# Two gated linear attention layers: half-chunk decay sums taken as rows, and a new order of work on three engines

## The chip, the cores and the metric

One core of a Trainium2 chip runs the whole program in one launch. The metric is device time in microseconds of one execution. Before the change three runs took 3049.61, 3051.63 and 3058.26 us.

## The reference

The program computes eight residual blocks on x of 2048 tokens by 128 features: an attention, a gated linear attention with experts (`L0_ffn`), a second attention, `L0_ffn` again, a selective scan, a mixture of experts, a gated delta rule, and the mixture of experts again. The change is in `L0_ffn` alone, which occurs twice with the same weights. Cut to what matters:

```
q1, k1, v = x@Wq * s, x@Wk, x@Wv              # 8 heads of 64
q2 = x@Wqa@Wqb * s ;  k2 = softmax(x@Wka@Wkb)
gk1 = log_sigmoid(x@Wg1a@Wg1b + bg1) / 16     # log decays <= 0
gk2 = log_sigmoid(x@Wg2a@Wg2b + bg2) / 16
e = softmax(x@We) ; one of 4 experts per token: mask, weight
chunk_gla(q, k, v, gk):                       # chunks of 64 tokens
    g = cumsum(gk) in the chunk ; qg = q*exp(g) ; kg = k*exp(-g)
    o = tril(qg kg^T) v  +  qg S
    S = S * exp(g_last) + (k*exp(g_last-g))^T v
o = chunk_gla(q1,k1,v,gk1) + sum over experts of
    chunk_gla(q2*w_e, k2*w_e, v, gk2*mask_e)
o = o * rsqrt(mean(o*o) + eps) * norm_w * silu(x@Wga@Wgb)
x = x + o @ Wo
```

## The kernel before, in words

`gla_ffn` (from line 790) handles the 2048 tokens in 16 tiles of 128. Its state has five parts: one dense and one for each of four experts. The kernel centres the cumulated log decays on the middle of a tile: `cum` sums them from the middle row. What crosses from one tile to the next is then the state times the exponential of the second half sum of the last tile and the first half sum of this one. These two half sums, for 512 key columns and five states, are the subject of the change.

- `halves(t)` (line 998, TensorE): for each of four groups of 128 key columns the log decays `gk` are the stationary operand (128x128 float32), and two columns (dense) or eight columns (four experts, two halves) stream past. That is eight small matrix products a tile, each of two passes, and they put the key columns on partitions, where `state_decay` needs them. The first four lie between `intra` and the expert part of `inter`, the last four between that and `update`.
- `exp_half(t)` (line 1440, ScalarE) takes the exponential of 128x40 numbers; `state_decay(t)` (line 1287, VectorE) multiplies the second half of the last tile with the first half of this one; `decay_state(t)` (POOL) scales the state by it.

Every engine has its program order written out by hand in the loops over t at the ends of `on_pe`, `on_dve`, `on_act`; semaphores join them. While tile t is finished, the front of tile t+1 is made (values, keys, queries, their decays) and the gate logits of t+2. TensorE's loop, in the names that are used below: `scores(t,0)` (line 1040, dense), `cumulate(t+1)` (988), `scores(t,1)` (experts), `spread_experts(t)` (1057, the expert mask over all partitions), `values`, `low_keys`, `low_queries`, `inter(t,(0,))` (1066, the old state's part of the output), `gate_logit(t+2,0)` and `(t+2,1)` (975), `gate_project(t+1)` (965), `intra(t)` (1083), halves, `inter(t,1..4)`, halves, `update(t,0)`, `update(t,1)` (1093), `keys`, `queries`, `sum_squares` (1108), `turn_k0`, `turn_q0` (transposes, 1019), `update_dense` (1100), `turn_k1`, `turn_q1`, `project` (1113).

VectorE's loop: `state_decay`, `mask_scores(t,0)`, `mask_scores(t,1)` (1292), `mask_queries(t)` (1300, 2048 columns), `subtract_max`, `normalise_keys`, `expert_queries`, `finish_gates(t+2)` (1241), `weigh_gate(t+1)` (1236), `add_state` twice, `decay_keys`, `dense_queries`, `add_state_dense`, `normalise`, `add_x`.

PSUM: three banks serve as a ring, whose order of uses is the list `TILE_USES`; a use may start when the reader of the use three places ahead of it has finished. `Dbank`, an eighth bank, holds in turn the spread masks, the output gate's logits (read by `weigh_gate`), and the dense part of the state's update.

```
TILE_USES = "cum0 cum1 klow v q2 half g0 g1 k1 q1 rs tk0 tq0 tk1 tq1 out".split()
```

In tiles 2 to 4 masks of later tokens are turned and multiplied as well, at the end of tile 1 VectorE chooses the experts of the last 1536 tokens, and in tile 0 the norm of the last 1024 tokens is finished.

## Time and profile before

| | |
|---|---|
| median of three runs | 3051.63 us |
| the profiled execution's own time | 3046.48 us |
| its span, first to last instruction | 3045.0 us |
| TensorE busy | 2802.7 us (92%) |
| VectorE busy | 2489.2 us (82%) |
| ScalarE busy | 2064.8 us (68%) |
| POOL busy | 858.6 us (28%) |
| first linear attention, start of its norm to its last x | 656.2 to 1068.7 us |
| second one, its last x | 2133.3 us |
| ScalarE exp_halves, line 1443 | 32 of 185 ns |

In a row of the timeline the first number is the start in us, the second the busy time of the group, then engine (PE a matmul, PEld its weight load), line, operation, output <- inputs, shapes and count, and in brackets the idle time ahead of it with what ended it. A float32 product shows as two weight loads and two matmuls. PEld's starts are the surest clock of TensorE's order: the time from the first load of one step to the first load of the next is what the step takes.

### The profile page before, as it was taken

Reading aid. Unit: us, or ns where it says so; the run is one execution under the profiler, and the core shown is the slowest. Engines: PE = TensorE matmul, PEld = TensorE weight load, DVE = VectorE, ACT = ScalarE, POOL = GpSimd, SP = SyncE. Lnnn points to the kernel's source line nnn. Section 1 sums busy time; section 2 is a strip of 40 time slices with the busy share of each in tenths; the row PEclk is TensorE's granted clock in tenths of the full one; section 3 lists DMA queues with packets and bytes.
Section 4 is the critical chain, followed back from the end, with each engine's and each line's share of the span. In section 5 each row is a group of like instructions: output and inputs, shape, how many; then the busy total and the mean of one; then the engine's idle time right before and its main releaser. Section 6 shows DMA issues by size and latency. Waiting matters only on the chain.

```text
span 3045.0 us, 58029 instructions
## 1 busy us (share of the span) xinstructions
PE 2802.7 (92%) x23121; PEld 1300.0 (43%) x23124; DVE 2489.2 (82%) x3245; ACT 2064.8 (68%) x3904; POOL 858.6 (28%) x1027
## 2 busy tenths in 40 slices
PE   7999999989999989999999899999887798678889
PEld 2222222236666622222222366666333365357655
DVE  8999999966666699999999666666799955899854
ACT  6999999965555469999999555554776423645232
POOL 1000000013333310000000133333388562199800
PEclk9999999989999989999999899999899999889989
DMA  2000000000000010000000000000000000000000
GB/s 92 10 17 16 16 17 16 11 6 1 2 2 1 2 53 11 16 16 16 16 17 11 11 1 2 1 2 2 26 0 0 10 1 1 0 1 1 1 1 14
DMA packets 29148, 33.62 MB, mean 11 GB/s; under 512 B 13195, under 2 KB 23438, under 8 KB 28622
## 3 DMA queue, kind: packets, MB, share of 16 engines
q1 hardware_dynamic: 28878, 29.92, 3.4%
q8 instruction: 182, 2.98, 0.4%
q14 instruction: 88, 0.72, 0.1%
HBM read 17.58 MB, written 7.34 MB: 8 GB/s over the span
## 4 chain that ended last, share of the span: by engine, by line
PE 69%; DVE 19%; ACT 6%; issue 3%; POOL 2%; DMA 0%; POOLq 0%; SPq 0%; DVEq 0%; another core or an unknown queue 0%; PEldq 0%; ACTq 0%
PE banks L391 15%; PE banks L373 10%; PE banks L366 6%; DVE max_parts L509 5%; PE banks L1078 3%; PE banks L2100 2%; PE banks L2085 2%; PE banks L1022 2%; PE banks L2087 2%; PE banks L1053 2%; PE banks L996 2%; PE banks L1097 2%; ACT probs L625 2%; DVE banks L2907 2%; DVE state_keys L2904 2%
## 5 line engine op out<-in xcount | busy, mean ns | idle before, releaser
L509 DVE TENSOR_REDUCE max_parts<-banks 128x2 f32<-128x1024 f32 x1024 | 1170.4, 1217 | 7.4 <-PE banks L366 6.7
L625 ACT ACTIVATE probs<-banks 128x512 f32<-128x512 f32 x2048 | 1085.0, 600 | 57.0 <-PE banks L373 30.3
L373 PE MATMUL banks<-q_parts,k_parts 51*128 51x512 bf16 x2048 | 654.0, 384 | 5.3 <-ACT v_heads L584 1.5
L391 PE MATMUL banks<-probs,v_heads 128*9 128x256 f32 x8192 | 637.5, 382 | 8.2 <-ACT pv_copy L636 2.0
L366 PE MATMUL banks<-k_parts,q_parts 48*128 48x512 bf16 x2048 | 593.9, 384 | 9.1 <-DVE max_parts L509 6.3
L373 PEld LDWEIGHTS banks<-q_parts,k_parts 51*128 51x128 bf16 x2048 | 151.8, 94 | 474.4 <-ACT probs L625 399.6
L692 POOL CAST neg_max_parts<-neg_max 128x8 bf16<-128x8 f32 x64 | 12.9, 202 | 1118.6 <-DVE neg_max L514 1118.6
L391 PEld LDWEIGHTS banks<-probs,v_heads 128*9 128x9 f32 x8192 | 123.2, 88 | 381.6 <-issue 342.9
L1635 POOL TENSOR_TENSOR state_times_c<-state,c_row 128x1024 f32<-128x1024 f32 x63 | 147.9, 2354 | 88.8 <-ACT c_row L1950 53.7
L1828 DVE TENSOR_TENSOR_SCAN state<-banks,state_carry,state 128x512 f32<-128x512 f32 x128 | 157.3, 1271 | 7.6 <-ACT banks L1945 5.5
L2264 ACT ACTIVATE silu_a<-banks 128x512 f32<-128x512 f32 x80 | 47.7, 597 | 162.9 <-PE banks L2085 162.7
L1713 PE MATMUL banks<-state_times_c,ident 128*128 128x512 f32 x256 | 131.4, 638 | 28.8 <-POOL state_times_c L1635 28.4
L906 POOL TENSOR_TENSOR state_middle<-state_end,state_decay 128x1280 f32<-128x1280 f32 x32 | 74.6, 2331 | 227.5 <-DVE state_decay L1290 227.5
L366 PEld LDWEIGHTS banks<-k_parts,q_parts 48*128 48x128 bf16 x2048 | 124.2, 93 | 33.4 <-DVE max_parts L509 20.0
L2160 DVE TENSOR_TENSOR hidden<-silu_a,banks 128x512 f32<-128x512 f32 x80 | 54.8, 687 | 88.3 <-PE banks L2087 84.6
L1945 ACT ACTIVATE banks<-dt,neg_A 128x512 f32<-128x512 f32 x128 | 86.1, 687 | 45.7 <-DVE state L1828 44.2
L2860 PE MATMUL banks<-state_queries,ident 128*128 128x256 f32 (+2 forms) x272 | 75.5, 443 | 41.7 <-POOL state_queries L2839 41.7
L2833 POOL TENSOR_TENSOR state_decayed<-state,decay 128x512 f32<-128x512 f32 x64 | 109.9, 1717 | 12.3 <-DVE state L2913 10.9
L1437 ACT ACTIVATE exp_cum<-banks 128x512 f32<-128x512 f32 x64 | 38.5, 601 | 90.5 <-PE banks L996 90.5
L2100 PEld LDWEIGHTS banks<-ffn_weights,hidden 128*128 128x128 f32 x640 | 85.1, 196 | 28.8 <-issue 23.5
L911 POOL TENSOR_TENSOR scores_dense<-scores_dense,scores_expert 128x1024 f32<-128x1024 f32 x32 | 75.7, 2365 | 75.0 <-DVE scores_expert L1297 75.0
L1475 ACT ACTIVATE out_square<-banks,eps_ln 128x512 f32<-128x512 f32 x32 | 22.1, 690 | 103.6 <-PE banks L1111 103.6
(511 smaller groups left out, 5122.6 us busy)
## 6 DMA issues: line engine op xcount, KB each, us to landing
outT_half<-pv_copy SPq DMA_DIRECT2D x248, 16.0 KB
prob_sums<-pv_copy SPq DMA_DIRECT2D x248, 2.0 KB
q_scratch<-qk_parts SPq DMA_DIRECT2D x8, 384.0 KB, 2.6
k_scratch<-qk_parts SPq DMA_DIRECT2D x8, 384.0 KB, 2.7
k_parts<-k_scratch SPq DMA_DIRECT2D x28, 96.0 KB
q_parts<-q_scratch SPq DMA_DIRECT2D x28, 96.0 KB
q_parts<-neg_max_rows SPq DMA_DIRECT2D x128, 3.0 KB
ffn_weights<-moe SPq DMA_DIRECT2D x1, 1928.0 KB, 7.6
```

What stands on the lines that cost most here:

```text
L366: nc.tensor.matmul(Mb[m % 2][:, blk(x)], Q[p % 2][half_of(x, ROWS), tile(t)], K[p % 2][half_of(x, ROWS), blk(b)], start=True, stop=True).t ...
L373: nc.tensor.matmul(bank("exp", n, x)[:, :], K[p % 2][half_of(x, ROWS + PARTS), tile(t)], Q[p % 2][half_of(x, ROWS + PARTS), blk(j)], start ...
L391: i = nc.tensor.matmul(PVb[group:group + VD, cols], V[:, t + k, 2 * (s // NB) + x, :], PT[:, (n + k) % RING, x, cols], start=(t == 0 and c ...
L509: nc.vector.tensor_reduce(mxp[s % 2][:, :, u // NB, u % NB], Mb[m % 2].rearrange("p (x k) -> p x k", x=2), AX.X, ALU.max).then_inc(*maxed. ...
L625: nc.scalar.activation(PT[:, n % RING, x, :], bank("exp", n, x)[:, :], ACT.Exp, scale=float(HD) ** -0.5).then_inc(*exped.inc())
L1078: i = nc.tensor.matmul(Obank[x][half_of(p), tile(yy)], SS[half_of(x), y, s, :], qT[t % 2][half_of(x), 0, y, :] if s == 0 else qm[half_of(x ...
L1635: nc.gpsimd.tensor_tensor(G[m % 2][:, :, :], F[m % 3][:, :, :], Cs[m % 2][:, :].unsqueeze(1).broadcast_to([128, 2, 512]), ALU.mult).then_i ...
L1713: nc.tensor.matmul(Yb[c][:, :], g.ident[:, :], G[m % 2][:, c, :], start=(n == 0), stop=(n == NS - 1)).then_inc(*summed.inc())
L1828: nc.vector.tensor_tensor_scan(f, decay_bank(m, c)[:, :], f, carry[:, c, n:n + 1], ALU.mult, ALU.add).then_inc(*scanned.inc())
L1945: nc.scalar.activation(decay_bank(m, c)[:, :], dt[:, c, unit_blk(m)], ACT.Exp, scale=negA[:, c, m % NS:m % NS + 1]).then_inc(*decay_made.i ...
L2100: i = nc.tensor.matmul(Yb(r)[:, tile(c)], hs[:, r % 3, tile(c)], w["w2"][:, u, :], start=(u in first and c == 0), stop=(u in last), skip_g ...
L2833: nc.gpsimd.tensor_tensor(SD[:, :, :, :], S[1 - s % 2][:, :, :, 0:HD], d, ALU.mult).then_inc(*decayed.inc())
```

## The change

The log decays become the moving operand. `halves(t)` is now two products: a 128x32 mask (one dense slot in use) against the 512 columns of `gk1` into partitions 0 to 31 of a bank, and a 128x32 mask (four experts, two halves in slots of eight) against `gk2` into partitions 32 to 63. ScalarE takes the exponential of these 64x512 numbers, and a new step `turn_halves(t)` turns them by four 64x128 transposes into columns 256 to 511 of `Dbank`. `state_decay` reads them there, and a new copy on VectorE keeps the second half for the next tile. POOL clears and fills the two masks once a layer. TensorE's, VectorE's and ScalarE's orders and the ring's list change too.

```diff
-TILE_USES = "cum0 cum1 klow v q2 half g0 g1 k1 q1 rs tk0 tq0 tk1 tq1 out".split()
+TILE_USES = "cum0 cum1 rows v q2 klow g0 g1 k1 q1 rs tk0 tq0 tk1 tq1 out".split()
...
-            def halves(t, pairs):
-                pe.wait_ge(*bank_read("half", t))
-                for pr in pairs:
-                    o = bank("half", t)[:, pr * 16:pr * 16 + 10].rearrange("p (k s) -> p k s", s=ST)
-                    nc.tensor.matmul(o[:, :, 0], gk[t % 2][:, 0, tile(pr)], g.half_col[:, :], start=True, stop=True)
-                    i = nc.tensor.matmul(o[:, :, 1:ST], gk[t % 2][:, 1, tile(pr)], half[:, t, :, :], start=True, stop=True)
+            def halves(t):
+                pe.wait_ge(*bank_read("rows", t))
+                pe.wait_ge(masks_begun, 3)
+                nc.tensor.matmul(bank("rows", t)[0:32, :], half_dense[:, :, :].rearrange("p s x -> p (s x)"), gk[t % 2][:, 0, :], start=True, stop=True)
+                nc.tensor.matmul(bank("rows", t)[32:64, :], half[:, t, :, :].rearrange("p s x -> p (s x)"), gk[t % 2][:, 1, :], start=True, stop=True).then_inc(*halves_made.inc())
+
+            def turn_halves(t):
+                pe.wait_ge(halves_exped, t + 1)
+                pe.wait_ge(second_kept, t)
+                pe.wait_ge(q_masked, t)
+                pe.wait_ge(gate_made, t + 1 if t else 0)
+                for r in range(4):
+                    i = nc.tensor.transpose(Dbank[:, 256 + 64 * r:320 + 64 * r], eh_rows[:, tile(r)], g.ident[0:64, 0:64])
+                i.then_inc(*halves_turned.inc())
...
                 scores(t, 0)
+                spread_experts(t)
                 if after:
                     cumulate(t + 1)
+                    halves(t + 1)
                 scores(t, 1)
-                spread_experts(t)
...
                 inter(t, (0,))
+                if after:
+                    gate_project(t + 1)
                 if t + 2 < NT:
                     gate_logit(t + 2, 0)
                     gate_logit(t + 2, 1)
-                if after:
-                    gate_project(t + 1)
                 intra(t)
-                if after:
-                    halves(t + 1, (0, 1))
                 inter(t, (1, 2, 3, 4))
-                if after:
-                    halves(t + 1, (2, 3))
...
                     turn_k0(t + 1)
                     turn_q0(t + 1)
                 if after:
+                    turn_halves(t + 1)
                     update_dense(t)
...
             def state_decay(t):
-                dve.wait_ge(exp_halves, t + 1)
+                dve.wait_ge(halves_turned, t + 1)
                 dve.wait_ge(decayed, t)
-                nc.vector.tensor_tensor(dec[:, :, :], eh[1 - t % 2][:, :, 1, :], eh[t % 2][:, :, 0, :], ALU.mult).then_inc(*decay_made.inc())
+                dve.wait_ge(second_kept, t)
+                nc.vector.tensor_tensor(dec[:, :, :], eh[1 - t % 2][:, :, :], turned_halves[:, :, :, 0], ALU.mult).then_inc(*decay_made.inc())
+                dve.wait_ge(decay_made, t)
+                nc.vector.tensor_copy(eh[t % 2][:, :, :], turned_halves[:, :, :, 1]).then_inc(*second_kept.inc())
...
+            state_decay(0)
             for t in range(NT):
                 after = t + 1 < NT
-                state_decay(t)
                 mask_scores(t, 0)
+                mask_queries(t)
                 mask_scores(t, 1)
-                mask_queries(t)
...
                 if after:
-                    weigh_gate(t + 1)
-                if after:
                     add_state(t, 0)
                     add_state(t, 1)
                     decay_keys(t + 1)
                     dense_queries(t + 1)
+                    weigh_gate(t + 1)
+                normalise(t)
                 if after:
                     add_state_dense(t)
-                normalise(t)
+                    state_decay(t + 1)
                 add_x(t)
...
             def exp_half(t):
                 act.wait_ge(halves_made, t + 1)
-                act.wait_ge(decay_made, t)
-                nc.scalar.activation(eh[t % 2][:, :, :, :].rearrange("p r k s -> p r (k s)"),
-                                     bank("half", t)[:, 0:64].rearrange("p (r x) -> p r x", r=4)[:, :, 0:10], ACT.Exp, scale=1 / 16.0).then_inc(*exp_halves.inc())
+                act.wait_ge(halves_turned, t)
+                nc.scalar.activation(eh_rows[:, :], bank("rows", t)[0:64, :], ACT.Exp, scale=1 / 16.0).then_inc(*halves_exped.inc())
...
                     exp_cumulated(t + 1)
+                    exp_half(t + 1)
...
                 square(t)
-                if after:
-                    exp_half(t + 1)
                 rms(t)
```

TensorE, middle of a tile, before: from the dense scores to the first half sums (two of the four pairs that follow `intra`, and the four after `inter`, are alike).

```order
L1053 MATMUL banks<-q_decayedT_139,k_decayedT_141 128x128 x8
L996 MATMUL banks<-log_decay_146,cum 128x512
L996 MATMUL banks<-log_decay_146,same_expert_cum 128x512
L1053 MATMUL banks<-q_decayedT_139,k_decayedT_141 128x128 x8
L1062 MATMUL banks<-expert_mask_rows,expert_select 128x128 x4
L983 MATMUL banks<-ffn_weights,xnT 128x512
L988 MATMUL banks<-ffn_weights,low_rank_qk 128x512
L1013 MATMUL banks<-ffn_weights,low_rank_qk 128x512
L1078 MATMUL banks<-q_decayedT_139,state_middle 64x128 x8
L979 MATMUL banks<-ffn_weights,low_rank_gates 128x512 x2
L972 MATMUL banks<-low_rank_gates,ffn_weights 128x128 x4
L1091 MATMUL banks<-scores_dense,v_tile_132 64x128 x8
```

The same place now:

```order
L1067 MATMUL banks<-q_decayedT_141,k_decayedT_143 128x128 x8
L1077 MATMUL banks<-expert_mask_rows,expert_select 128x128 x4
L1004 MATMUL banks<-log_decay_148,cum 128x512
L1004 MATMUL banks<-log_decay_148,same_expert_cum 128x512
L1009 MATMUL banks<-log_decay_148,half_dense 32x512
L1010 MATMUL banks<-log_decay_148,half_mask 32x512
L1067 MATMUL banks<-q_decayedT_141,k_decayedT_143 128x128 x8
L991 MATMUL banks<-ffn_weights,xnT 128x512
L996 MATMUL banks<-ffn_weights,low_rank_qk 128x512
L1027 MATMUL banks<-ffn_weights,low_rank_qk 128x512
L1093 MATMUL banks<-q_decayedT_141,state_middle 64x128 x8
L980 MATMUL banks<-low_rank_gates,ffn_weights 128x128 x4
```

The spread masks have moved ahead of the cumulated sums, the half sums ahead of the expert scores, and the gate's projection ahead of the gate logits, which come next.

TensorE, end of a tile, now (before, L1018's row, `turn_halves`, is not there and all else stands in this order):

```order
L1126 MATMUL banks<-out_square,head_ones 128x512
L1036 MATMUL banks<-ident,k_decayed_140 128x128 x4
L1036 MATMUL banks<-ident,q_decayed 128x128 x4
L1018 MATMUL banks<-ident,exp_half_rows 128x64 x4
L1120 MATMUL banks<-v_tile_134,k_decayed_139 64x64 x8
L1036 MATMUL banks<-ident,k_decayed_140 128x128 x4
L1036 MATMUL banks<-ident,q_decayed 128x128 x4
L1132 MATMUL banks<-ffn_weights,outT_tile 128x128 x4
```

The new transposes wait for `weigh_gate`, since they write into the bank that it reads, and five steps are queued behind them.

VectorE, from the gates to the next tile's masks, before:

```order
L1245 SCALAR_TENSOR_TENSOR log_decay_145<-banks,abs_logit 128x512
L1239 SCALAR_TENSOR_TENSOR out_gateT_130<-banks,ffn_weights,gate_sigmoid 128x512
L1310 TENSOR_TENSOR state_end<-state_middle,banks 128x2x256 x2
L1275 TENSOR_TENSOR k_decayed_138<-banks,exp_neg_cum 128x512
L1285 SCALAR_TENSOR_TENSOR q_decayed<-banks,exp_cum 128x512
L1315 TENSOR_TENSOR state_end<-state_middle,banks 128x4x64
L1320 TENSOR_TENSOR outT_tile<-outT_tile,out_square 128x512
L1324 TENSOR_TENSOR x_tok<-x_tok,banks 128x128
L1290 TENSOR_TENSOR state_decay<-exp_halves_143,exp_halves_144 128x20
L1297 TENSOR_TENSOR scores_dense<-banks,tri 128x512 x2
```

And now:

```order
L1300 SCALAR_TENSOR_TENSOR q_decayed<-banks,exp_cum 128x512
L1254 SCALAR_TENSOR_TENSOR out_gateT_132<-banks,ffn_weights,gate_sigmoid 128x512
L1338 TENSOR_TENSOR outT_tile<-outT_tile,out_square 128x512
L1333 TENSOR_TENSOR state_end<-state_middle,banks 128x4x64
L1306 TENSOR_TENSOR state_decay<-exp_second_half_145,banks 128x20
L1308 COPY exp_second_half_146<-banks 128x20
L1342 TENSOR_TENSOR x_tok<-x_tok,banks 128x128
L1315 TENSOR_TENSOR scores_dense<-banks,tri 128x512 x2
L1322 TENSOR_TENSOR q_experts<-q_decayedT_142,banks 128x2048
L1315 TENSOR_TENSOR scores_expert<-banks,same_expert_tri 128x512 x2
```

`weigh_gate` (out_gateT) follows the queries, the norm goes ahead of the dense state, the new copy stands behind the decay, and the queries' mask stands between the two masks of the scores.

## Rows read from the trace of the kernel before

**Rows 1.** Windows: engines busy (records), TensorE's granted clock, DMA share and GB/s.

```profile
656.00:695.07 39.07, 31.70 (x106) 17.99 (x107) 21.16 (x80) 18.66 (x37) 6.82 (x19) 0.63 0.03 7
846.35:1029.68 183.33, 183.15 (x1858) 122.70 (x1857) 122.42 (x192) 106.46 (x192) 69.09 (x56) 1.00 0.01 2
```

**Rows 2.** Timeline of TensorE's weight loads, one whole tile of layer one.

```profile
846.35 0.97 PEld L1053 LDWEIGHTS banks<-q_decayedT,k_decayedT 64*128 64x128 f32 x16
847.44 0.30 PEld L996 LDWEIGHTS banks<-log_decay,cum 128*128 128x128 f32 x2
...
849.36 0.97 PEld L1053 LDWEIGHTS banks<-q_decayedT,k_decayedT 64*128 64x128 f32 x16 [0.76 <-DVE scores_dense L1297]
...
851.83 0.18 PEld L988 LDWEIGHTS banks<-ffn_weights,low_rank_qk 64*128 64x128 f32 x1 [0.76 <-issue]
...
852.89 0.43 PEld L1078 LDWEIGHTS banks<-q_decayedT,state_middle 64*64 64x64 f32 x16 [0.76 <-issue]
853.49 0.58 PEld L979 LDWEIGHTS banks<-ffn_weights,low_rank_gates 17*128 17x128 f32 x4 [0.17 <-issue]
854.83 0.96 PEld L972 LDWEIGHTS banks<-low_rank_gates,ffn_weights 64*128 64x128 f32 x8 [0.76 <-DVE q_experts L1304]
...
856.93 0.30 PEld L1002 LDWEIGHTS banks<-half_col,log_decay 128*128 128x128 f32 x2 [0.17 <-DVE k_stats L1260]
...
859.83 0.30 PEld L1002 LDWEIGHTS banks<-half_col,log_decay 128*128 128x128 f32 x2 [0.17 <-issue]
...
860.82 1.49 PEld L1097 LDWEIGHTS banks<-v_experts,k_decayed 128*64 128x64 f32 x16
862.70 0.30 PEld L1009 LDWEIGHTS banks<-ffn_weights,xnT 128*128 128x128 f32 x2 [0.39 <-ACT exp_halves L1443]
...
865.71 0.47 PEld L1022 LDWEIGHTS banks<-ident,q_decayed 128*128 128x128 f32 x4
866.34 0.55 PEld L1105 LDWEIGHTS banks<-v_tile,k_decayed 128*64 128x64 f32 x16 [0.17 <-issue]
866.96 0.42 PEld L1022 LDWEIGHTS banks<-ident,k_decayed 128*128 128x128 f32 x4
867.52 0.42 PEld L1022 LDWEIGHTS banks<-ident,q_decayed 128*128 128x128 f32 x4
868.15 0.97 PEld L1117 LDWEIGHTS banks<-ffn_weights,outT_tile 128*128 128x128 f32 x8 [0.22 <-DVE outT_tile L1320]
869.24 0.30 PEld L1053 LDWEIGHTS banks<-q_decayedT,k_decayedT 64*128 64x128 f32 x4
```

**Rows 3.** The page, groups: the attentions' products with nine stationary columns.

```profile
L391 PE MATMUL banks<-probs,v_heads 128*9 128x256 f32 x8192 | 637.5, 382 | 8.2 <-ACT pv_copy L636 2.0
```

**Rows 4.** Timeline of ScalarE in the same tile.

```profile
853.03 0.69 ACT L1427 ACTIVATE q_decayed<-banks,expert_weight_scaled 128x512 f32<-128x512 f32 x1 [0.51 <-PE banks L1013]
...
855.93 1.06 ACT L1410 ACTIVATE abs_logit<-banks 128x512 f32<-128x512 f32 x2
...
861.55 0.63 ACT L1471 ACTIVATE out_square<-outT_tile 128x512 f32<-128x512 f32 x1
```

**Rows 5.** Timeline of VectorE in the same tile.

```profile
851.76 2.28 DVE L1304 TENSOR_TENSOR q_experts<-q_decayedT,banks 128x2048 f32<-128x2048 f32 x1
...
859.22 1.28 DVE L1245 SCALAR_TENSOR_TENSOR log_decay<-banks,abs_logit 128x512 f32<-128x512 f32 x2
861.02 0.75 DVE L1239 SCALAR_TENSOR_TENSOR out_gateT<-banks,ffn_weights,gate_sigmoid 128x512 f32<-128x512 f32 x1 [0.51 <-ACT gate_sigmoid L1404]
861.95 0.69 DVE L1310 TENSOR_TENSOR state_end<-state_middle,banks 128x512 f32<-128x512 f32 x1 [0.18 <-PE banks L1097]
...
864.72 0.69 DVE L1285 SCALAR_TENSOR_TENSOR q_decayed<-banks,exp_cum 128x512 f32<-128x512 f32 x1 [0.17 <-PE banks L1017]
```

**Rows 6.** Timeline of TensorE's weight loads: the expert scores of tile 2.

```profile
752.59 0.29 PEld L1053 LDWEIGHTS banks<-q_decayedT,k_decayedT 64*128 64x128 f32 x2 [1.22 <-DVE scores_dense L1297]
```

**Rows 7.** Timeline of VectorE in tile 15, the last.

```profile
1055.35 1.29 DVE L1297 TENSOR_TENSOR scores_expert<-banks,same_expert_tri 128x512 f32<-128x512 f32 x2 [1.04 <-PE banks L1053]
```

More of the change, by code:

```diff
@@ L844, in gla_ffn @@
         readers = dict(g0=(gates_made, 2, 1), g1=(gates_made, 2, 2), v=(v_copied, 1, 1), klow=(k_steps, 7, 2), rs=(sums_log, 1, 1), gp=(gate_made, 1, 1),
-                       cum0=(exp_cums, 2, 1), cum1=(exp_cums, 2, 2), half=(exp_halves, 1, 1), out=(x_added, 1, 1), k1=(k_decayed, 1, 1),
+                       cum0=(exp_cums, 2, 1), cum1=(exp_cums, 2, 2), rows=(halves_exped, 1, 1), out=(x_added, 1, 1), k1=(k_decayed, 1, 1),
                        q2=(q_kept, 1, 1), tk1=(k1T, 1, 1), q1=(q_dense, 1, 1), tk0=(k0T, 1, 1), tq1=(q1T, 1, 1), tq0=(q0T, 1, 1),
@@ L1499, in on_act @@
             norm.deviation(3)
-            act.wait_ge(zeroed, 1)
             exp_half(0)
```

34 lines of the change are left out of this document (21 added, 13 removed).

## Prediction

> **What bounds the kernel now.** I read the table of the page first: TensorE is busy for 92% of the span, but that is a mean over stages. The windows come next: over eight tiles of the first linear attention (846.35 to 1029.68 us) TensorE is busy for 183.15 of 183.33 us at the full granted clock (level 2.4 GHz), the others for two thirds at most [rows 1]. So here a gain is what TensorE's list of steps loses, as long as no other engine is made later than TensorE. The weight loads tell what each step takes: a tile runs from dense scores to dense scores, 846.35 to 869.24, 22.89 us [rows 2]. What I want from these rows is which of the 22.89 us is streaming, and which a wait; the idle time in brackets alone does not say it.
>
> - The low-rank keys and queries (two products that run side by side on half the rows) take 851.83 to 852.89, 1.06 us. Two 512-column products one behind the other take 847.44 to 849.36, 1.92 us. So one stream of 512 float32 columns is 0.86 us, and a change of shape costs about 0.2 [rows 2].
> - The two gate logits are built to run side by side as well, but take 853.49 to 854.83, 1.34 us: 0.28 more. The second one's bank is freed by the copy of the queries, which ends at 853.03 + 0.69 = 853.72, after the logits have begun [rows 2, 4]. This is a wait of 0.28.
> - Four transposes take 865.71 to 866.34 = 0.63 with a change of shape, so 0.44 without; the pair from 866.96 to 867.52 takes 0.56, a wait of 0.12 (a bank that ScalarE's copy frees). The last four take 867.52 to 868.15, 0.63 with no change of shape: 0.19 is a wait for the norm on VectorE, as its bracket says [rows 2].
> - The 0.39 in front of the keys, put down to exp_halves, is no wait: `update` streams 16 passes of 256 columns in pairs, 8 x 0.215 = 1.72, with a change of shape 1.9, and 860.82 to 862.70 is 1.88 [rows 2]. Removing exp_halves from there gains nothing.
>
> Waits to be had: 0.28 + 0.12 + 0.19 = 0.59 us a tile.
>
> **The change, part by part (one tile).**
>
> 1. *Removed: eight small products.* The second four take 859.83 to 860.82 = 0.99, changes of shape included; the first four, from 856.93 on, are alike. **-1.98**.
> 2. *Added: two products of 512 columns with 32 stationary columns each.* If they run side by side they cost one stream and one change of shape, 0.86 + 0.2 = 1.06; one after the other 1.92. The attentions have such products, with nine stationary columns in groups of 32: 8192 records, 637.5 us busy [rows 3]. A 256-column pass streams for 0.215 us (512 columns, two passes, 0.86), so in a row they would need 8192 x 0.215 = 1761 us. They plainly overlap. I take **+1.06**.
> 3. *Added: four transposes of 64 rows.* No row has this form. Below: update_dense, eight 64-column products in 866.34 to 866.96, 0.62 with its change of shape, so half its stream, 0.21, and 0.2: 0.41. Above: weight load and stream one after the other. A load's record is near 0.14 (0.47 busy for four overlapping ones) and 64 columns stream in about 0.05, so 4 x 0.19 + 0.2 = 0.97. In the nearest row, four transposes of 128 columns from 865.71 on, they take 0.11 each although each load alone is longer than that: loads run under streams. I take the same 0.44, as a load of 128 columns is needed here too, and 0.19 for the change of shape: **+0.63** [rows 2]. The Trainium skill has a rule against this step (TensorE: Matmul & The Clock Gate, Part 3, "The mechanism"): a weight load overlaps a matmul in flight only where the row group differs, and these four share one. By that rule the sum would take the upper end, 0.97, and the gain would be 10 us smaller; the rows speak against it for full-height tiles, none shows 64 rows.
> 4. *Moved: gate projection ahead of the logits.* The logits then begin 1.09 later (eight loads, as 846.35 to 847.44), when the queries are copied: **-0.28**. The projection needs the masked queries, and `mask_queries` is now ahead of the expert masks, so they are ready some 3 us early.
> 5. *Moved: norm ahead of the dense state; the new step between turn_q0 and turn_k1.* Both end waits of TensorE (0.12 and 0.19) are then covered, since its transposes and projection arrive 0.63 later: **-0.31**.
> 6. *At nothing:* the exponential of 64x512 instead of 128x40 (0.6 instead of 0.2 on ScalarE, which has over 1 us free between the cumulated sums and the values), VectorE's copy of 128x20 (0.2, in the wait for the projection), POOL's masks (before the routing needs them), and the spread masks' new place, which has as many changes of shape as before.
>
> Sum: -1.98 + 1.06 + 0.63 - 0.28 - 0.31 = **-0.88 us a tile**, a period of 22.01.
>
> **Does another engine become late?** Times from a tile's dense scores. TensorE: spread 1.09, sums 1.42, halves 3.33, expert scores 4.39, values 5.48, low rank 6.54, old state 7.60, projection 8.20, logits 9.29, intra 10.35. From the end of the projection to `update` was 4.90 (855.92 to 860.82), of which 1.98 goes: update 13.27, keys 15.15, new transposes 13.27 + 5.52 = 18.79 [rows 2]. The logits are now the latest input of ScalarE. It reads them 1.20 after their first load (851.83 to 853.03), at 10.49, and was at 855.93, 9.58: **0.9 us later, while TensorE is 1.2 earlier at its end of this part**. The squares are done 6.25 after (855.93 to 862.18): 16.74; the sum of squares can use them at 16.97. VectorE: gates from 10.49 + 3.29 = 13.78 (855.93 to 859.22), 1.28, two additions and the keys at 0.69 each: 17.13. Queries from keys + 2.02 = 17.17, 0.69, gate 0.75: 18.65 with a hand-over [rows 2, 4, 5]. The new transposes wait for that gate and begin at 18.79. So both chains arrive 0.1 to 0.2 ahead. This is the thin place of the change: slack of over 2 us at the squares is used up.
>
> **Edges, per layer.** Tile 2: choosing experts makes VectorE late, and the expert scores begin 3.47 after the dense ones (749.12 is 0.46 more than the usual 3.01 before 752.59) and run 0.6 longer; now they begin at 4.39 anyway: -1.06 [rows 6]. Tile 15: with `mask_queries` (2.28) ahead of the expert mask, which waited 1.04 for its scores, the mask comes 1.24 later, POOL's sum and the output behind it: +1.2 [rows 5, 7]. Before tile 0 TensorE runs at a mean granted clock of 0.63 [rows 1], at 1.2 GHz for much of it; the half sums cost about the same there, the new transposes up to twice 0.63: I take +0.8, bounds 0 and 1.4.
>
> Fifteen tiles a layer have the new form: 15 x -0.88 - 1.06 + 1.2 + 0.8 = -12.3, two layers **-24.6 us**. Against the profiled execution, 3046.48, that is 3021.9; the median of the runs is 5.15 above that execution, so I forecast 3051.63 - 24.6 = **3027.0**.
>
> **The rivals.** About 0.3% (9 us) is what a measurement can tell.
>
> - *The new transposes load and stream in turn*: 0.97 instead of 0.63, 30 x 0.34 = 10 us back: 3037. For it: no row has this height. Against: the full-height transposes [rows 2]. 0.10. The Trainium skill's rule above (TensorE: Matmul & The Clock Gate, Part 3) would have it so.
> - *The chain through the late logits sets the period by a little*: every 0.1 us a tile costs 3 us. The slack is 0.1 to 0.2 over a dozen hand-overs. At 0.3 us over: 3036; up to 0.6: 3045. For it: the slack. Against: every link is taken with its hand-over from a row. 0.15, of which 0.03 ends within 0.3%.
> - *The two half sums run one after the other*: +0.86 a tile, 30 x 0.86 = 25.8: the change does not do what it says, no change at 3053. Rows 3 are against it. 0.08.
> - *Slower: VectorE's gate becomes the end of the tile.* Place: `weigh_gate` behind `dense_queries`, with new transposes, dense update, four steps more and the next scores queued behind it on TensorE. It decides once the chain from the logits to this gate (18.65 - 9.29 = 9.36 us) grows by more than 0.14; it undoes all gain at 1.0 and is slower by over 0.3% from about 1.3. At 1.5 longer: 30 x 1.36 = 41 less 24.6, 3068. For it: ScalarE may be behind by its longer exponential and by one more step. Against: before, gates ended at 860.50 and VectorE then waited 0.5, 0.2 and 0.2. 0.05.
>
> **How the numbers follow.** Forecast 0.62. Faster: 0.62 + 0.10 + 0.12 = 0.84; within 0.3%: 0.08 + 0.03 = 0.11; slower 0.05. Low end: transposes at 0.41 (-6.6), no loss before tile 0 (-1.6), a spread of runs of 3: 3016. High end: up to the chain at 0.5 us over, 3042, which leaves out the serial half sums, the slower case and a little below.
>
> **What would show it.** In the changed profile a middle tile's period of 22.0; the half sums' two kinds of weight loads within 0.02 us of each other, and the expert scores 1.06 behind them; the logits' step 1.06; the new transposes 0.63 to the dense update's first load; no wait for the square or the gate. A period of 22.35 with 0.97 there is the first rival, one of 22.9 with 1.92 for the half sums the third; a wait of TensorE for the gate or for out_square the second or fourth. Wrong altogether is a gain that comes with these steps unchanged, from another stage.

## The result, and the profile after

The changed kernel takes **3021.76 us** (median of 4 runs, 3016.84 to 3022.55), the kernel before 3052.66 in the same comparison: ratio 0.9897, 95% interval 0.9883 to 0.9911. The medians differ by 30.9 us, the two profiled executions' spans by 24.1 (3045.0 to 3020.9); forecast was 24.6, and 3027.0 for the median. The total is near the forecast, but as the rows show, by errors of opposite sign.

The page of the changed kernel, its table of busy time:

```profile
PE 2776.3 (92%) x22868; PEld 1246.2 (41%) x22868; DVE 2508.1 (83%) x3277; ACT 2083.7 (69%) x3904; POOL 860.4 (28%) x1033
```

TensorE is busy for 26 us less, VectorE and ScalarE for 19 us more each. Eight tiles of the first linear attention, as windows (columns as in [rows 1]):

```profile
842.87:1016.00 173.13, 173.13 (x1795) 108.64 (x1794) 127.64 (x200) 111.15 (x192) 68.98 (x57) 1.00 0.01 2
```

Eight tiles take 173.13 us where they took 183.33 [rows 1], TensorE still without a gap at full granted clock. A tile takes **21.64 us instead of 22.89**. TensorE's weight loads in one tile, against [rows 2]:

```profile
842.87 0.97 PEld L1067 LDWEIGHTS banks<-q_decayedT,k_decayedT 64*128 64x128 f32 x16
...
846.20 0.11 PEld L1009 LDWEIGHTS banks<-log_decay,half_dense 128*32 128x32 f32 x1 [0.76 <-issue]
846.21 0.11 PEld L1010 LDWEIGHTS banks<-log_decay,half_mask 128*32 128x32 f32 x1
...
847.18 0.97 PEld L1067 LDWEIGHTS banks<-q_decayedT,k_decayedT 64*128 64x128 f32 x16 [0.84 <-issue]
...
850.99 0.96 PEld L980 LDWEIGHTS banks<-low_rank_gates,ffn_weights 64*128 64x128 f32 x8 [0.17 <-issue]
852.07 0.30 PEld L987 LDWEIGHTS banks<-ffn_weights,low_rank_gates 17*128 17x128 f32 x4
853.13 0.85 PEld L1106 LDWEIGHTS banks<-scores_dense,v_tile 128*64 128x64 f32 x16 [0.76 <-issue]
...
856.06 1.49 PEld L1112 LDWEIGHTS banks<-v_experts,k_decayed 128*64 128x64 f32 x16 [0.17 <-issue]
857.94 0.30 PEld L1023 LDWEIGHTS banks<-ffn_weights,xnT 128*128 128x128 f32 x2 [0.38 <-issue]
...
859.56 0.40 PEld L1126 LDWEIGHTS banks<-out_square,head_ones 128*128 128x128 f32 x2 [0.46 <-ACT out_square L1488]
860.19 0.14 PEld L1036 LDWEIGHTS banks<-ident,k_decayed 128*128 128x128 f32 x1 [0.24 <-issue]
...
860.95 0.47 PEld L1036 LDWEIGHTS banks<-ident,q_decayed 128*128 128x128 f32 x4
861.59 0.33 PEld L1018 LDWEIGHTS banks<-ident,exp_half_rows 64*128 64x128 f32 x4 [0.17 <-issue]
861.98 0.55 PEld L1120 LDWEIGHTS banks<-v_tile,k_decayed 128*64 128x64 f32 x16
862.59 0.42 PEld L1036 LDWEIGHTS banks<-ident,k_decayed 128*128 128x128 f32 x4
862.98 0.47 PEld L1036 LDWEIGHTS banks<-ident,q_decayed 128*128 128x128 f32 x4
863.42 0.97 PEld L1132 LDWEIGHTS banks<-ffn_weights,outT_tile 128*128 128x128 f32 x8
864.51 0.97 PEld L1067 LDWEIGHTS banks<-q_decayedT,k_decayedT 64*128 64x128 f32 x16
```

- Half sums: both kinds load within 0.01 us, and the expert scores begin 0.98 behind them (847.18 - 846.20).
- From intra to update 2.93 us (856.06 - 853.13), before 4.90 [rows 2]: -1.97.
- Projection and logits 2.14 (853.13 - 850.99), before 2.43 [rows 2]: -0.29.
- New transposes 0.39 (861.98 - 861.59).
- From the transposed queries to the next scores 3.56 (864.51 - 860.95), before 3.53 [rows 2]; without the new step that is 3.17: -0.36.

Sum: -1.97 + 0.98 - 0.29 + 0.39 - 0.36 = -1.25, the whole difference of the periods.

The bracket at 859.56 names out_square, but from keys to transposes is 2.25 (860.19 - 857.94), as from 862.70 [rows 2] to this load before the change, so it costs nothing:

```profile
864.95 0.14 PEld L1022 LDWEIGHTS banks<-ident,k_decayed 128*128 128x128 f32 x1 [0.24 <-issue]
```

The 0.39 of the new transposes holds two things. Their four loads, 0.14 us each, take 0.33 together, so they follow each other every 0.06 us, and from the last one to the next step's first is 0.21:

```profile
861.77 0.14 PEld L1018 LDWEIGHTS banks<-ident,exp_half_rows 64*128 64x128 f32 x1
```

The late chains arrive as the prediction has them: VectorE's gate ends at 861.31, 0.28 ahead of the new transposes.

```profile
853.23 1.09 ACT L1428 ACTIVATE abs_logit<-banks 128x512 f32<-128x512 f32 x2 [0.66 <-PE banks L987]
...
858.88 0.63 ACT L1488 ACTIVATE out_square<-outT_tile 128x512 f32<-128x512 f32 x1
```

```profile
856.55 1.28 DVE L1260 SCALAR_TENSOR_TENSOR log_decay<-banks,abs_logit 128x512 f32<-128x512 f32 x2
...
860.57 0.74 DVE L1254 SCALAR_TENSOR_TENSOR out_gateT<-banks,ffn_weights,gate_sigmoid 128x512 f32<-128x512 f32 x1
```

(ScalarE's and VectorE's timelines of the same tile.) From the tile's start at 842.87 the logits are read at 10.36 (forecast 10.49), the squares done at 16.64 (16.74), the gate at 18.44 (18.65).

**The edges** went otherwise. Laid out per layer, from the norm's first statistics to the next stage's, worked out from the starts of the dense scores of each tile:

| first layer, us | before | after | forecast | measured |
|---|---|---|---|---|
| norm to tile 0 | 38.85 | 38.27 | (with tile 0) | -0.58 |
| tile 0 | 31.17 | 32.39 | -0.88 + 0.8 | +1.22 |
| tiles 1 to 14 | 325.59 | 306.98 | 14 x -0.88 - 1.06 | -18.61 |
| tile 15 to the end | 17.11 | 21.29 | +1.2 | +4.18 |
| sum | 412.72 | 398.93 | -12.3 | -13.79 |

The second layer has 412.16 and 398.94. Both together give 27.0 us, 2.4 more than forecast; the first layer also began 2.8 us later in this execution (659.00, before 656.22), in stages that the change does not touch, which leaves the 24.1 of the spans. That the spans come within 0.5 us of the forecast is in part this chance. The two executions are also no typical pair: that of the kernel before, 3046.48, is shorter than all four of the comparison (3049.61 and up), that of the changed kernel, 3022.55, the longest of its four.

TensorE's matmuls in tile 15, and two windows there (columns as in [rows 1]):

```profile
1044.99 1.98 PE L1106 MATMUL banks<-scores_dense,v_tile 128*64 128x128 f32 x16 [4.06 <-POOL scores_dense L919]
1046.90 3.64 PE L1093 MATMUL banks<-q_experts,state_middle 64*64 64x128 f32 x64
```

```profile
1041.00:1045.00 4.00, 0.01 (x2) 0.01 (x2) 1.52 (x3) 0.00 (x0) 2.34 (x1) 0.82 0.00 0
1045.00:1049.00 4.00, 4.00 (x56) 3.67 (x60) 0.00 (x0) 0.00 (x0) 0.00 (x0) 0.50 0.02 4
```

The wait for POOL's sum is 4.06 us (before 2.68), as the later mask has it. Then the granted clock is 0.50 (1.2 GHz), and the expert part takes 3.64 instead of 1.98. Before, the same two steps ran at full clock:

```profile
1059.12 1.09 PE L1091 MATMUL banks<-scores_dense,v_tile 128*64 128x128 f32 x16 [2.68 <-POOL scores_dense L911]
1060.15 1.98 PE L1078 MATMUL banks<-q_experts,state_middle 64*64 64x128 f32 x64
```

Ahead of tile 0 TensorE has a new wait, in tile 0 another, and 1.2 GHz sets in between them:

```profile
693.67 0.46 PE L1018 MATMUL banks<-ident,exp_half_rows 64*128 64x64 f32 x4 [1.62 <-ACT exp_half_rows L1461]
...
699.99 0.60 PE L1077 MATMUL banks<-expert_mask_rows,expert_select 4*128 4x128 bf16 x4 [0.61 <-DVE exp_second_half L1308]
```

```profile
695.40:705.60 10.20, 8.82 (x34) 4.25 (x32) 4.82 (x10) 5.43 (x10) 2.33 (x1) 0.50 0.01 2
```

The kernel before has a stretch at 1.2 GHz of the same length there, but it ends 3.8 us after tile 0's dense scores (695.07), where this one lasts 8.3 us into tile 0 (697.27). A window of the kernel before:

```profile
688.60:698.90 10.30, 9.53 (x44) 7.74 (x44) 5.63 (x16) 5.62 (x13) 1.10 (x1) 0.50 0.01 2
```

### The profile page after: what moved, and what is told of

Read it like the earlier page. It is cut to its first block, busy times and chain, and to the rows that moved or that the text cites. A ratio compares the mean times of both kernels' runs of the same rounds, so it can differ in the third digit from the quotient of the medians.

```text
span 3020.9 us, 57613 instructions
## 1 busy us (share of the span) xinstructions
PE 2776.3 (92%) x22868; PEld 1246.2 (41%) x22868; DVE 2508.1 (83%) x3277; ACT 2083.7 (69%) x3904; POOL 860.4 (28%) x1033
## 4 chain that ended last, share of the span: by engine, by line
PE 67%; DVE 20%; ACT 6%; issue 4%; POOL 3%; DMA 0%; POOLq 0%; SPq 0%; DVEq 0%; another core or an unknown queue 0%; PEldq 0%; ACTq 0%
PE banks L391 15%; PE banks L373 10%; DVE max_parts L509 7%; PE banks L366 5%; PE banks L1093 3%; PE banks L2115 2%; PE banks L1004 2%; PE banks L2100 2%; PE banks L2102 2%; PE banks L1067 2%; PE banks L1112 2%; PE banks L1036 2%; ACT probs L625 2%; DVE banks L2922 2%; DVE state_keys L2919 2%
## 5 line engine op out<-in xcount | busy, mean ns | idle before, releaser
L2115 PE MATMUL banks<-ffn_weights,hidden 128*128 128x128 f32 x640 | 86.4, 280 | 2.3 <-DVE hidden L2175 1.3
```

Of the source, the lines that this page charges most:

```text
L2115: i = nc.tensor.matmul(Yb(r)[:, tile(c)], hs[:, r % 3, tile(c)], w["w2"][:, u, :], start=(u in first and c == 0), stop=(u in last), skip_g ...
```

## The experiments

Ratios are to the kernel before, whose median was 3052.66 beside the changed kernel and 3051.29 (e1 to e4), 3051.65 (e5 to e8) and 3052.3 (e9, e10) in the three later groups of runs. "Period" is from dense scores to dense scores of a middle tile, "tail" from tile 15's dense scores to the next stage's first statistics, in both layers; "tile 0" is that of the first layer.

| kernel | median us | ratio, interval | period | tile 0 | tails |
|---|---|---|---|---|---|
| after | 3021.76 | 0.9897, 0.9883 to 0.9911 | 21.64 | 32.39 | 21.29, 21.24 |
| e1_same_group | 3044.93 | 0.9978, 0.9969 to 0.9987 | 22.49 | 30.58 | 21.34, 19.41 |
| e2_third_group | 3019.99 | 0.9902, 0.9888 to 0.9917 | 21.65 | 32.67 | 21.34, 20.98 |
| e3_tail | 3017.70 | 0.9898, 0.9881 to 0.9915 | 21.64 | 32.25 | 18.47, 20.11 |
| e4_best | 3009.84 | 0.9872, 0.9856 to 0.9889 | 21.64 | 28.13 | 17.00, 20.19 |
| e5_logits_first | 3028.14 | 0.9921, 0.9902 to 0.9940 | 21.91 | 31.70 | 20.37, 19.81 |
| e6_gate_early | 3036.31 | 0.9948, 0.9928 to 0.9967 | 22.17 | 32.76 | 19.98, 21.06 |
| e7_norm_late | 3027.48 | 0.9919, 0.9903 to 0.9935 | 22.00 | 31.69 | 19.52, 19.34 |
| e8_masks_old | 3047.31 | 0.9989, 0.9964 to 1.0014 | 22.24 or 23.85 | 28.74 | 18.41, 18.37 |
| e9_order_alone | 3046.64 | 0.9979, 0.9969 to 0.9989 | 22.61 | 29.57 | 18.47, 18.30 |
| e10_last_spread | 3007.51 | 0.9854, 0.9840 to 0.9868 | 21.64 | 28.14 | 16.99, 20.08 |

### Do the two half sums run side by side? (e1, e2)

Each adds one product of 512 columns with 32 stationary columns; e1 into the rows of the first, e2 into rows that nothing else writes:

```diff
                 nc.tensor.matmul(bank("rows", t)[0:32, :], half_dense[:, :, :].rearrange("p s x -> p (s x)"), gk[t % 2][:, 0, :], start=True, stop=True)
+                nc.tensor.matmul(bank("rows", t)[0:32, :], half_dense[:, :, :].rearrange("p s x -> p (s x)"), gk[t % 2][:, 0, :], start=True, stop=True)
```

and for e2 in its place

```diff
+                nc.tensor.matmul(bank("rows", t)[64:96, :], half_dense[:, :, :].rearrange("p s x -> p (s x)"), gk[t % 2][:, 0, :], start=True, stop=True)
```

> The changed kernel with the dense half sums computed twice into the same partitions 0 to 31 (the second overwrites the first with the same numbers). Theory (two half sums side by side, because they lie in different column groups; one stream each is 0.86 us): the repeat lies in the group of the first and queues behind it, so the step from half sums to expert scores grows from 0.98 to 1.84 us, the period of a middle tile from 21.64 to about 22.5, and 32 such steps make the kernel 27 us slower than the changed kernel, near 3049. Rival (the step is bounded by something else than the streams of a group, so that the products are cheap in any place): 0 to 5 us.

> The changed kernel with the dense half sums computed a second time into partitions 64 to 95 of the same bank, which nobody reads. Theory (column groups side by side): the same extra work as in the run before, in an idle group, costs about 0.01 us a tile; the step stays at 0.98 to 1.0 us, the kernel within 2 us of the changed one. Rival (three streams of 128 rows share one path and take turns): 0.86 us a tile, 27 us.

TensorE's weight loads in a middle tile of e1, then of e2:

```profile
846.76 0.11 PEld L1009 LDWEIGHTS banks<-log_decay,half_dense 128*32 128x32 f32 x1 [0.76 <-issue]
846.77 0.11 PEld L1011 LDWEIGHTS banks<-log_decay,half_mask 128*32 128x32 f32 x1
...
847.22 0.11 PEld L1010 LDWEIGHTS banks<-log_decay,half_dense 128*32 128x32 f32 x1 [0.31 <-issue]
...
848.60 0.41 PEld L1068 LDWEIGHTS banks<-q_decayedT,k_decayedT 64*128 64x128 f32 x6 [0.84 <-issue]
```

```profile
845.17 0.11 PEld L1009 LDWEIGHTS banks<-log_decay,half_dense 128*32 128x32 f32 x1 [0.76 <-issue]
845.17 0.11 PEld L1010 LDWEIGHTS banks<-log_decay,half_dense 128*32 128x32 f32 x1
845.18 0.11 PEld L1011 LDWEIGHTS banks<-log_decay,half_mask 128*32 128x32 f32 x1
...
846.16 0.86 PEld L1068 LDWEIGHTS banks<-q_decayedT,k_decayedT 64*128 64x128 f32 x14 [0.84 <-issue]
```

The same product costs 0.86 us (1.84 instead of 0.98, period +0.85) where the first product's 32 columns are taken, and 0.01 in 32 free ones. The rival of serial half sums is out. By the medians e1 is 23 us slower than the changed kernel, not the expected 27; its first layer had a fast tile 0 by chance, as e4 below shows.

### What each move is worth (e5, e6, e7, e9)

e5 puts the logits ahead of the gate projection again:

```diff
                 inter(t, (0,))
-                if after:
-                    gate_project(t + 1)
                 if t + 2 < NT:
                     gate_logit(t + 2, 0)
                     gate_logit(t + 2, 1)
+                if after:
+                    gate_project(t + 1)
```

> The changed kernel with the gate logits ahead of the gate projection again. Theory (the logits lost 0.28 us to the queries' copy, and the late logits make the chain over ScalarE tight, without setting the period): the logits' step is 1.34 instead of 1.06 us, the wait of the sum of squares for the square (0.46 in brackets, 0 in the steps' times) goes, and the period rises from 21.64 by about 0.28: 28 tiles, 8 us slower than the changed kernel. Rival (the chain through the late logits sets the period): the earlier logits make up for the wait or more, and the period is the same or shorter.

Period +0.27. The term of 0.28 is right. And since ScalarE now reads the logits 0.75 us earlier (9.61 us from the dense scores instead of 10.36) and nothing else is gained by it, the chains through the late logits do not set the changed kernel's period.

e6 puts VectorE's gate, 0.75 us, ahead of the additions and the keys again:

```diff
+                    weigh_gate(t + 1)
                     add_state(t, 0)
                     add_state(t, 1)
                     decay_keys(t + 1)
                     dense_queries(t + 1)
-                    weigh_gate(t + 1)
```

> The changed kernel with weigh_gate ahead of the two state additions again. Theory (that place was moved because the sigmoid now ends late): VectorE waits there some 0.5 us for the sigmoid, then spends 0.75 us, and the keys, which TensorE's transposes wait for and which had 0.2 to 0.3 us of slack, come about 1 us late: the period rises by 0.7 to 1.2 us, 20 to 36 us slower. Rival (VectorE is free between these steps, since it follows TensorE there; the place is worth nothing): the period stays at 21.64.

Period +0.53. TensorE's weight loads wait twice, for keys and for queries:

```profile
861.89 0.42 PEld L1036 LDWEIGHTS banks<-ident,k_decayed 128*128 128x128 f32 x4 [0.98 <-DVE k_decayed L1290]
862.49 0.42 PEld L1036 LDWEIGHTS banks<-ident,q_decayed 128*128 128x128 f32 x4 [0.18 <-DVE q_decayed L1300]
```

VectorE waits for the sigmoid as before the change, and its keys come later by that wait too:

```profile
859.30 0.75 DVE L1254 SCALAR_TENSOR_TENSOR out_gateT<-banks,ffn_weights,gate_sigmoid 128x512 f32<-128x512 f32 x1 [0.51 <-ACT gate_sigmoid L1422]
...
861.16 0.68 DVE L1290 TENSOR_TENSOR k_decayed<-banks,exp_neg_cum 128x512 f32<-128x512 f32 x1
```

From the tile's dense scores the keys begin at 17.33 us (843.83 to 861.16) instead of 16.24 in the changed kernel: 1.09 later, as expected. Their transposes begin at 18.06 instead of 17.32, 0.74 later, so the slack ahead of them was 0.35 and not 0.2 to 0.3. Another 0.2 comes back behind them: keys to queries takes 0.60 instead of 0.76. This is why the period rose by 0.53, below the expected 0.7 to 1.2. It is the slack of the keys, not that of the gate or the squares, which the prediction worked out.

e7 puts VectorE's norm behind the dense state again:

```diff
-                normalise(t)
                 if after:
                     add_state_dense(t)
+                normalise(t)
+                if after:
                     state_decay(t + 1)
```

> The changed kernel with the dense state's addition ahead of the norm again. Theory: the dense update now ends 0.39 us later than it would without the new transposes, the addition waits for it and the norm for the addition, and the projection, whose first load is at 5.48 us after the keys', could begin only at about 6.0: the period rises by 0.5 us, 15 us slower. Rival (the projection has slack): nothing.

Period +0.37 (expected 0.5); TensorE's projection waits 0.34 for outT_tile. This is the wait of 0.19 that the prediction removes, and it would have grown.

e9 is the kernel before with its eight small products, and three of the moves alone:

```diff
                 scores(t, 0)
+                spread_experts(t)
...
                 scores(t, 1)
-                spread_experts(t)
...
                 inter(t, (0,))
+                if after:
+                    gate_project(t + 1)
...
                 mask_scores(t, 0)
+                if after:
+                    mask_queries(t)
                 mask_scores(t, 1)
-                mask_queries(t)
+                if not after:
+                    mask_queries(t)
```

> The kernel before, with its eight small half-sum products, but with three of the moves: the spread masks' product ahead of the cumulated sums, mask_queries ahead of the expert mask (not in the last tile), the gate projection ahead of the logits. My theory (the logits' wait of 0.28 for the copy of the queries is all that these moves take away; the rest of the gain comes from the half sums as rows): middle period 22.89 - 0.28 = 22.6 (22.4 to 22.7), logits' step 1.06, the waits of 0.12 and 0.19 at the transposes as before; 28 or 30 tiles x 0.28 = 8 us, median near 3043. Rival (the moves are what gains, the form of the half sums little): period under 22.2, median under 3032. Second rival (the moves gain nothing alone, since the logits come later and the chain through them ends at the gate): period 22.8 to 22.9, median 3050 or more.

Period 22.61, -0.28: the logits' wait and no more. Over both layers its profiled execution is 10.2 us shorter than the kernel before (407.46 and 407.25 instead of 412.72 and 412.16): about 1.6 a layer are gained in tile 0, and 1.4 a layer lost in the tail (18.47 and 18.30 instead of 17.11 and 16.86), where the granted clock falls as in the changed kernel. The median fell by 5.7 only; that execution, 3034.98, was the shortest of 12 that reach to 3052.15, and what lengthened the others no profile shows. By the periods the moves give 0.28 of the 1.25; the other 0.97 comes with the half sums as rows and VectorE's order behind them.

### The mask order inside the loop (e8)

```diff
                 scores(t, 0)
-                spread_experts(t)
...
                 scores(t, 1)
+                spread_experts(t)
...
                 mask_scores(t, 0)
-                mask_queries(t)
                 mask_scores(t, 1)
+                mask_queries(t)
```

> The changed kernel with the spread masks behind the expert scores and the expert mask ahead of the queries' mask again, in all tiles. Theory: the queries' mask then ends 2.28 us later, at about 9.2 us from the dense scores, while the gate projection, which writes into the same bank, could begin at 8.2: TensorE waits 1 us there, 30 us slower in all, less the 8 us that the last tiles give back: 15 to 25 us slower than the changed kernel. Rival (the wait is hidden): only the 8 us less.

The gate projection then waits 0.6 a tile for the masked queries (expected 1.0). In the first layer that is nearly all: period 22.24, one tile apart. In the second the granted clock falls in ten of the tiles 1 to 14, eight of them in a row. Two windows of one tile, columns as in [rows 1]:

```profile
1905.00:1912.00 7.00, 6.47 (x56) 3.48 (x54) 4.92 (x6) 2.85 (x6) 4.28 (x4) 1.00 0.00 0
1912.20:1915.70 3.50, 3.50 (x52) 3.17 (x54) 3.04 (x7) 3.44 (x5) 0.57 (x1) 0.51 0.03 5
```

TensorE's matmuls there: intra 1.74 us instead of 1.02 a step, the expert part 2.81 instead of 1.91. Such a tile takes 23.85, 1.61 more than 22.24 with the same order. That the clock would fall was not expected: the expected 15 to 25 us were for a wait of 1.0, and came about with 0.6 and the clock. This goes with the spread of its ten runs, 3034.4 to 3066.1, and with an interval that takes in no change. The median is 25.6 us above the changed kernel's: most of the change's gain hangs on the places of two masks' steps, 0.6 us a tile as a wait and the rest through the clock. The edit moves one step on TensorE and one on VectorE; no run tells them apart.

### The edges (e3, e4, e10)

e3 gives the last tile the old mask order on VectorE:

```diff
                 mask_scores(t, 0)
-                mask_queries(t)
+                if after:
+                    mask_queries(t)
                 mask_scores(t, 1)
+                if not after:
+                    mask_queries(t)
```

> The changed kernel, but in the last tile of each layer the expert mask goes ahead of the queries' mask again. Theory: the last tile's queries' mask delays the expert mask by 1.24 us, TensorE's wait for POOL's sum grows from 2.68 to 4.06 us, and in that wait the granted clock falls to 1.2 GHz, so the rest of the tile runs at half speed: both go, the stretch from the last dense scores to the last x shrinks from 21.1 (second layer) to about 16.7 us, 8 us less in all, near 3014. Rival (the clock falls there for another reason, such as the earlier stretch of long streams with 32 columns): only the 1.24 us come back, 2.5 us in all, and TensorE's expert part still takes 3.6 us instead of 2.0.

TensorE's wait falls from 4.06 to 3.00, the tails to 18.47 and 20.11. It is not the 17.1 of before, since the granted clock still falls to 1.2 GHz in both layers: the theory was right in the wait and wrong in the clock. Two windows behind the wait, one of each layer:

```profile
1042.40:1045.60 3.20, 2.78 (x32) 2.45 (x36) 0.13 (x1) 0.00 (x0) 0.36 (x1) 0.50 0.00 0
2086.80:2093.50 6.70, 5.23 (x80) 4.87 (x80) 1.18 (x1) 0.00 (x0) 1.41 (x1) 0.50 0.01 2
```

e3's median is 4 us below the changed kernel's, with intervals that overlap: by the medians it is not told apart, by the tails it is.

e4 is e3, and in the preparation of tile 0 ScalarE's exponential of the halves moves ahead of the second softplus, the new transposes behind the first keys and queries, VectorE's state_decay ahead of the gate:

```diff
-            turn_halves(0)
             turn_k1(0)
             turn_q1(0)
+            turn_halves(0)
...
-            weigh_gate(0)
             dve.wait_ge(zeroed, 2)
             state_decay(0)
+            weigh_gate(0)
...
+            exp_half(0)
             softplus(1)
             norm.deviation(2)
             norm.deviation(3)
-            exp_half(0)
```

> The run before, with three more edits ahead of the first tile: ScalarE's exponential of the first half sums ahead of the softplus of tile 1, TensorE's first new transposes behind turn_q1, and VectorE's first state decay ahead of the first output gate. Theory: the wait of 1.8 us for that exponential (693.67) and the wait of 0.9 us for the kept second half (699.99) go, 1 to 2 us a layer, and if the stretch at 1.2 GHz that lasts to 705.6 in the changed kernel (to about 699 before the change) comes from those waits, it ends earlier, for up to 2 us more: 2 to 8 us under the run before. Rival (the slow stretch comes from the new order itself: the masks spread and 512-column streams first): the waits go, but the clock rises at the same point, and the gain is under 3 us in all.

TensorE's matmuls ahead of tile 0, and the window behind them:

```profile
690.08 0.46 PE L1018 MATMUL banks<-ident,exp_half_rows 64*128 64x64 f32 x4
...
693.75 0.39 PE L1077 MATMUL banks<-expert_mask_rows,expert_select 4*128 4x128 bf16 x4
```

```profile
692.70:702.00 9.30, 9.30 (x76) 5.07 (x78) 7.55 (x14) 5.64 (x11) 4.54 (x2) 1.00 0.01 2
```

Both waits are gone, and so is the stretch at 1.2 GHz: tile 0 takes 28.13 instead of 32.39, and the norm to tile 0 36.11 instead of 38.27, 6.4 us in the first layer and 5.8 in the second (1.30 and 4.48). How much of it is clock, e1 tells by chance. It waits at the same two places, 0.77 us for the exponential (its extra product fills the rest) and 1.53 for the copy, in both layers alike; its first layer ran at full clock there, its second did not. The spread of the masks in the first layer and in the second:

```profile
698.12 0.39 PE L1078 MATMUL banks<-expert_mask_rows,expert_select 4*128 4x128 bf16 x4 [1.53 <-DVE exp_second_half L1309]
...
1759.43 0.60 PE L1078 MATMUL banks<-expert_mask_rows,expert_select 4*128 4x128 bf16 x4 [1.53 <-DVE exp_second_half L1309]
```

```profile
694.00:704.00 10.00, 7.54 (x53) 3.80 (x51) 5.32 (x11) 5.70 (x11) 2.33 (x1) 1.00 0.01 2
```

(This window is the first layer's.) Its tile 0 takes 30.58 at full clock and 33.54 in the second layer: 2.96 us are the clock alone, and the same waits do not bring it down every time. Without the extra product of 0.85 it would be 29.73, which sets the changed kernel's 32.39 apart into 2.7 us of clock and 1.6 for the wait in tile 0, against e4. Against the kernel before less of it is new, since that one ran at 1.2 GHz there too, as shown above.

e10 is e4 with TensorE's spread of the masks behind the expert scores, in the last tile alone:

```diff
                 scores(t, 0)
-                spread_experts(t)
                 if after:
+                    spread_experts(t)
                     cumulate(t + 1)
                     halves(t + 1)
                 scores(t, 1)
+                if not after:
+                    spread_experts(t)
```

> As e4_best, and in the last tile alone the spread masks' product stands behind the expert scores again, as in the kernel before. In e4_best TensorE waited about 3.0 us there for the summed scores in both layers; the granted clock fell to 1.2 GHz there in the second layer (tail 20.19) and not in the first (17.00). Theory (the clock falls there because of how long TensorE waits; 2.68 as before is short enough): wait 2.6 to 2.8, no fall in either layer, both tails 16.8 to 17.2, span 3.2 us less than e4_best's 3003.9, near 3000.7. Rival (the wait's length does not decide between 2.7 and 3.0, and whether it falls hangs on something else): the wait shortens, the clock falls in one layer or both, tail 20 there, span 3003 to 3007.

TensorE's matmuls in tile 15 of the first layer and of the second, in e10:

```profile
1036.05 1.09 PE L1106 MATMUL banks<-scores_dense,v_tile 128*64 128x128 f32 x16 [2.68 <-POOL scores_dense L919]
...
2080.41 1.97 PE L1106 MATMUL banks<-scores_dense,v_tile 128*64 128x128 f32 x16 [2.69 <-POOL scores_dense L919]
```

The theory falls: the wait is 2.7 us again, as before the change, and the clock falls in the second layer (tail 20.08) and not in the first (16.99), as in e4. The same instructions with the same wait run at either clock. A wait's length between 2.7 and 3.0 does not decide it; what does stays open. The other tails say the same: the clock fell in both of e8's behind a wait of 2.68, in neither of the kernel before behind the same wait, and in all twelve tails of the kernels that keep the wait of 4.06 (the changed one, e1, e2, e5, e6, e7), which take 19.3 to 21.3 us. The two tails of e10 price the fall alone: 20.08 - 16.99 = 3.1 us. The intervals of e4 and e10 overlap, so the two are not told apart. Both medians lie below the changed kernel's, by 12 and 14 us; e10's interval lies wholly below its, e4's overlaps it a little.

## Why the prediction was right, and where it was not

**Right in its mechanism.** The bound is TensorE's list of steps; it fell by what the steps lost, and no other engine became the bound. Eight small products: -1.98, measured -1.97. Logits side by side: -0.28, measured -0.29 and again 0.27 in e5. The chains through the late logits were placed to 0.2 us, and e5 shows that they do not set the period. The slack of 0.1 to 0.2 itself no run tested: e6 puts its delay on the keys. Of the rivals, serial half sums fell with e1 and e2, the slower one and the chain by TensorE's steps without a wait.

**A term mis-sized: the new transposes.** The step took "+0.63": "the same 0.44, as a load of 128 columns is needed here too", and 0.19 for a change of shape. It measured 0.39, just below its own lower bound of 0.41. The length of a load does not set the pace: they follow each other every 0.06 us, where the full-height transposes of 128 columns stand 0.11 apart (0.47 us for four loads of 0.14 at 860.95). 0.06 is also the pace of the dense update's pairs (16 loads in 0.55 us), which stream 64 columns like these transposes; that speaks for the streams as what sets it, but no run varied the columns. Four times 0.06 and 0.15 for the change of shape behind them are the 0.39. The first rival, loads and streams in turn, would have taken 0.97 and is out. The Trainium skill's rule (TensorE: Matmul & The Clock Gate, Part 3, "The mechanism") is that a load overlaps a matmul in flight only where the row group differs. The trace does not agree with it here: 0.39, with the loads 0.06 apart.

**Smaller ones.** Half sums 0.98 instead of 1.06: a change of shape costs 0.12 there, not 0.2. The waits at the tile's end gave 0.36 instead of 0.31. Together with the transposes this is 0.24 + 0.08 + 0.05 = 0.37 a tile, 5.2 us over tiles 1 to 14 of a layer. Tile 2's own term of -1.06 measured -0.82 (25.36 to 23.29, less the 1.25 of every tile).

**The step that failed: the edges.** "So the mask comes 1.24 later, POOL's sum and the output behind it: +1.2." The wait did grow by 1.38. But the step priced only the wait, and what follows it ran at half clock: +4.18 in all. The same order gave +4.38 in the second layer and +2.4 to +4.2 in the other kernels that keep it, so this size is in part chance. Of tile 0 the prediction took "+0.8, bounds 0 and 1.4" for half sums and transposes at 1.2 GHz, on top of -0.88. It did not ask who waits for the *exponential* before the first tile, where nothing covers it. "At nothing: the exponential of 64x512" holds in the loop; ahead of tile 0 TensorE waits 1.62 for it, and in tile 0 0.61 for VectorE's copy. The new transposes ahead of tile 0 ran at full clock (0.39 us, 693.67 to 694.06); what ran at 1.2 GHz stands in tile 0, where the slow stretch now lies. With the preparation's -0.58 the measured sum is +0.64 instead of -0.08, so in the total it is the tail that was mis-sized most. e4 shows what another order ahead of tile 0 is worth, 6 us a layer.

So 5.2 us a layer more gained in the loop stand against 3.7 us more lost at the edges (first layer); both layers together came out at 27.0 us, and 2.8 us in untouched stages brought the spans to within 0.5 us of the forecast. That closeness is luck; the range would have held without it. The medians fell by 6 us more than the forecast; with medians of before from 3051.3 to 3052.7 and executions of the kernel before 8.65 us apart, this lies within what the runs scatter; no run was made for it.

## What to carry to other kernels

Lay a changed loop out as prologue, tiles and tail, and price each by itself: what a step costs at nothing in the loop stands open at its ends. Price a wait of TensorE at an edge from the wait alone up to the wait with the steps behind it at half clock. And where small products have the wide operand stationary, turn them over and put them into free column groups: a second one there cost 0.01 us, in the same group 0.86.

## What the runs showed of the hardware

- The granted clock fell in the tiles of e8's second layer with TensorE busy for 6.47 of 7.00 us ahead of the fall, and stayed at full level in nearly all tiles of its first layer with the same order. In e4 and e10 one and the same tail ran at either level, and so did e1's tile 0 with the same two waits in its two layers. The fall costs 0.7 to 1.7 us a step (e8's intra 1.74 instead of 1.02, the last tile's expert part 3.64 instead of 1.98), 3.0 us in e1's tile 0 and 3.1 in e10's tail.
- Four transposes with 64 rows in the same row group, streaming 64 columns each, took 0.39 us: their loads stand 0.06 us apart, though one load's record is 0.14 us long, and 0.15 more lies ahead of the next shape.
